# A gated attention and FFN block on one core: VectorE's order at the FFN entry, a third row buffer, and the first scores in banks of their own

## The chip, the cores and the metric

One core of a Trainium2 chip runs the kernel. The metric is the device time of one execution in microseconds. TensorE multiplies, VectorE and ScalarE read its results out of PSUM, GpSimd works on SBUF alone, SyncE issues most DMAs.

## The reference, cut to what matters

Eight batches of 100 rows of width 2048 attend to 722 context rows each, which serve as keys and as values. The result is added to x through a gate. Then a linear layer of 2048 by 2048, whose weights are packed with 6 bits each, is added through a second gate.

```python
a = einsum('bqd,bkd->bqk', layernorm(x), ctx)       # x: 8,100,2048   ctx: 8,722,2048
x = x + tanh(g_xattn[0]) * einsum('bqk,bkd->bqd', softmax(a), ctx)
w = (unpacked_6_bit(qweight) - zero_point) * scale  # 2048 x 2048
x = x + tanh(g_ffn[0]) * (einsum('bsd,nd->bsn', layernorm(x), w) + bias)
```

## The kernel before, in words

Every engine runs a program of its own, written out by hand; semaphores tie them together. What an engine does next is the order of the code in its block, and a wait at its head holds everything behind it on that engine.

**Split operands.** fp32 operands are split in a high part (rounded, made by ScalarE) and a low part (the rest, made by VectorE or GpSimd). Products are the sum of three passes: high by high, low by high, high by low.

**Attention, batch b.** `queries` turns the normalised rows of x (in `xa`) in four groups: TensorE transposes into a PSUM bank, ScalarE writes the high half of `qT` (L535), VectorE the low half (L877). `scores(b)` goes over 32 chunks f: TensorE turns three blocks of context (L980), ScalarE copies `khi` (L544), VectorE subtracts `klo` (`keys_lo`, L887), and three chunks later TensorE multiplies (L1025 with khi, L1027 with klo) into the two banks of `S`. VectorE takes the maximum (`row_max`), ScalarE the exponential (`exps`). `attend(b)` multiplies the probabilities with the context, six row tiles in the order of `ORDER` or `LAST_ORDER`, into the four `pv` banks (L1063, L1074). Its low operands `vlo` come from GpSimd (L487). VectorE adds the result to x piece by piece (`residual`, L764).
`keys_lo`, `keys_hi`, `scores`, `attend` and `multiply` take a table of hooks: other work that stands ahead of chunk or tile f. So the statistics of the next x (`ln1_stats`) stand at chunks 27 to 30 of batch 0, and the unpacking of weight tiles 0 and 1 (`unpack_piece`, five operations each) from chunk 12 on of batch 7.
The turns use four banks `T`: two of their own and, while batches 0 and 1 are loaded, `pv0` and `pv1` too. A bank is written again when its low half has been taken (`s_free`).

**FFN.** 800 rows are cut into row blocks of 128 and a tail of 32. A block m is read back from DRAM into a row buffer (`load_rows`, buffers in `XROW`), turned by TensorE in two halves of eight transposes (`normed`), copied by ScalarE (`rows_hi`, L607) and VectorE (`rows_lo`, L796). A weight tile n (128 of the 2048 outputs) is loaded (`load_w`), unpacked by VectorE (`unpack`, L817 to L824), turned by TensorE (`weights`, L1098, 16 transposes) and copied by ScalarE (L529). `multiply(nb, m)` is 16 steps of two matmuls (L1131). VectorE finishes each result tile j in two parts: `before(j)` prepares x1 (L853, L856; it needs the DMA of `load_x1` and of `rs_all`), `after(j)` combines it with the product (L868, L871).
`weights(n)` and the next `normed` share the banks T0 and T1, so TensorE's turns wait for VectorE's `rows_lo` of the block before.

**Start.** SyncE loads x[0] in four pieces, then 24 pieces of context of batch 0, x[1], and so on: all in one queue. TensorE turns the identity 34 times (L1159) before the first queries, after waiting for all masks of GpSimd.

The functions as they stand before:

## Time and profile before

| what | us |
| --- | --- |
| median of 3 runs (lowest, highest) | 606.73 (603.69, 607.91) |
| the profiled execution, its own time | 604.58 |
| its span, first to last instruction | 602.8 |
| TensorE busy | 576.8 (96%) |
| VectorE busy | 357.2 (59%) |
| ScalarE busy | 287.3 (48%) |
| GpSimd busy | 221.3 (37%) |

In the rows, PE is TensorE, PEld its weight loads, DVE VectorE, ACT ScalarE, POOL GpSimd, SPq the DMAs that SyncE issues. Lnnn is the line of the kernel. What stands in brackets is how long the engine was idle before the row and which engine or DMA ended that. PEclk is the granted TensorE clock: 1.00 is 2.4 GHz, 0.50 is 1.2 GHz.

### The profile page before, as it was taken

To read this page: it belongs to the slowest core of one execution; us is meant where nothing else is said; L and a number is where in the kernel's file an instruction comes from. 1 tells how busy PE (TensorE), PEld (TensorE's weight loads), DVE (VectorE), ACT (ScalarE), POOL (GpSimd) and SP (SyncE) were. 2 spreads that over 40 slices of the span, in tenths; PEclk is the share of its full clock that TensorE was granted. 3 is DMA by queue.
4 is the path that set the end of the run, shared out by engine and by line. 5 is a ranking of instruction groups with operands and counts; after the bars stand their busy time and mean duration, and the time that the engine had idled before them with its cause. 6 is when DMAs were issued, how large, how long until landed. Compare 5 with 4: busy or idle time off the path is not lost.

```text
span 602.8 us, 8793 instructions
## 1 busy us (share of the span) xinstructions
PE 576.8 (96%) x3458; PEld 413.1 (69%) x3458; DVE 357.2 (59%) x680; ACT 287.3 (48%) x450; POOL 221.3 (37%) x196
## 2 busy tenths in 40 slices
PE   7989999999999999999999899992999999999997
PEld 7968969968968968968968876651654444444445
DVE  5676717827827827826836946771757764654433
ACT  3755567568568568568568567441323211210000
POOL 2046178169169269269269159420000000000000
PEclk9998999999999999999999999996999999999999
DMA  7999649237847856846848485896434984972311
GB/s 231 280 271 255 202 135 316 73 114 222 226 154 223 200 184 222 232 147 229 216 159 296 108 314 211 241 261 176 151 134 140 262 242 113 207 152 62 89 53 39
DMA packets 44435, 113.69 MB, mean 189 GB/s; under 512 B 21026, under 2 KB 21282, under 8 KB 35778
## 3 DMA queue, kind: packets, MB, share of 16 engines
q1 hardware_dynamic: 27388, 108.12, 59.1%
q10 hardware_dynamic: 16750, 5.01, 5.2%
q8 instruction: 27, 0.44, 0.4%
q14 instruction: 14, 0.11, 0.1%
q0 software_dynamic: 256, 0.00, 0.0%
HBM read 89.26 MB, written 19.66 MB: 181 GB/s over the span
## 4 chain that ended last, share of the span: by engine, by line
PE 84%; DVE 6%; DMA 3%; POOL 3%; ACT 2%; issue 1%; SPq 0%; POOLq 0%; DVEq 0%; ACTq 0%
PE pv L1131 18%; PE pv L1063 13%; PE S L1025 13%; PE T L980 9%; PE S L1131 8%; PE S L1027 7%; PE pv L980 5%; PE pv L1074 5%; DVE xres L764 3%; POOL vlo L487 2%; DMA late<-x_scratch 2%; DMA raw<-in_L_ffn_qweight 1%; PE T L1098 1%; PE T L1159 1%; DVE qT L877 1%
## 5 line engine op out<-in xcount | busy, mean ns | idle before, releaser
L487 POOL TENSOR_TENSOR vlo<-raw,vhi 128x2048 fp32r<-128x2048 f32 (+1 forms) x38 | 175.4, 4644 | 50.3 <-ACT vhi L555 50.3
L1025 PE MATMUL S<-khi,qT 128*100 128x362 f32 x512 | 142.1, 359 | 2.2 <-ACT khi L544 2.2
L1027 PE MATMUL S<-klo,qT 128*100 128x362 f32 x256 | 85.8, 335 | 3.5 <-DVE klo L887 3.0
L1063 PE MATMUL pv<-vhi,ph 128*100 128x512 f32 (+1 forms) x304 | 85.4, 397 | 0.6 <-DVE xres L764 0.4
L887 DVE TENSOR_TENSOR klo<-pv,khi 128x361 fp32r<-128x361 f32 x128 | 65.1, 526 | 25.7 <-ACT khi L544 25.1
L887 DVE TENSOR_TENSOR klo<-T,khi 128x361 fp32r<-128x361 f32 x128 | 65.8, 529 | 23.2 <-ACT khi L544 22.5
L1131 PE MATMUL pv<-raw 128*128 128x512 f16 x352 | 78.0, 379 | 0.0
L544 ACT ACTIVATE khi<-T 128x361 fp32r<-128x361 f32 x128 | 58.4, 474 | 36.6 <-PE T L980 36.5
L555 ACT ACTIVATE vhi<-raw 128x2048 fp32r<-128x2048 f32 (+1 forms) x38 | 71.9, 1908 | 6.8 <-PE pv L1063 6.7
L544 ACT ACTIVATE khi<-pv 128x361 fp32r<-128x361 f32 x128 | 58.5, 476 | 28.3 <-PE pv L980 28.2
L1025 PEld LDWEIGHTS S<-khi,qT 128*100 128x100 f32 x512 | 68.3, 168 | 2.4 <-ACT E L579 2.4
L980 PE MATMUL T<-ident,raw 128*128 128x128 f32 (+2 forms) x432 | 66.7, 270 | 0.5 <-DVE qT L877 0.5
L1131 PEld LDWEIGHTS pv<-raw 128*128 128x128 f16 x352 | 34.2, 98 | 41.4 <-issue 1.7
L1063 PEld LDWEIGHTS pv<-vhi,ph 128*100 128x100 f32 (+1 forms) x304 | 49.3, 165 | 19.0 <-DVE xres L764 1.4
L980 PEld LDWEIGHTS T<-ident,raw 128*128 128x128 f32 (+2 forms) x432 | 55.7, 149 | 5.9 <-issue 1.3
L980 PE MATMUL pv<-ident,raw 128*128 128x128 f32 (+1 forms) x384 | 59.6, 266 | 0.0
L877 DVE TENSOR_TENSOR qT<-T,qT 128x400 fp32r<-128x400 f32 x28 | 14.8, 569 | 70.6 <-ACT qT L535 70.6
L980 PEld LDWEIGHTS pv<-ident,raw 128*128 128x128 f32 (+1 forms) x384 | 48.8, 140 | 3.7 <-DVE qT L877 0.7
L1027 PEld LDWEIGHTS S<-klo,qT 128*100 128x100 f32 x256 | 42.4, 166 | 8.8 <-DVE klo L887 8.2
L466 POOL TENSOR_SCALAR ln<-mr 100x1 f32<-100x1 f32 x16 | 3.7, 230 | 114.4 <-DVE mr L721 113.9
L1063 PE MATMUL pv<-vlo,ph 128*100 128x512 f32 (+1 forms) x152 | 44.6, 393 | 0.0
L626 ACT ACTIVATE xa<-raw 128x2048 f16<-128x2048 f16 x8 | 15.3, 1910 | 50.0 <-DVE raw L824 45.9
(110 smaller groups left out, 681.6 us busy)
## 6 DMA issues: line engine op xcount, KB each, us to landing
raw<-in_ctx SPq DMA_DIRECT2D x24, 1024.0 KB, 9.6
raw<-in_L_ffn_qweight SPq DMA_DIRECT2D x16, 768.0 KB, 7.2
raw<-in_ctx SPq DMA_DIRECT2D x12, 840.0 KB, 8.7
raw<-in_ctx SPq DMA_DIRECT2D x32, 256.0 KB, 10.9
xres<-in_x SPq DMA_DIRECT2D x8, 800.0 KB
x_scratch<-xres SPq DMA_DIRECT2D x8, 800.0 KB
rows_scratch<-xres SPq DMA_DIRECT2D x8, 800.0 KB
late<-x_scratch SPq DMA_DIRECT2D x24, 256.0 KB, 5.0
```

The costliest lines, as they stand in the source:

```text
L487: pool.tensor_tensor(vlo[0:r, k, :], raw[0:r, b % 2, t, :], vhi[0:r, k, :].bitcast(F32), ALU.subtract).then_inc(s_vlo, 1)
L544: act.activation(khi[:, (b * 2 * CH + f) % RING, 0:GW], T[k][:, 0:GW], ACT.Copy).then_inc(s_khi, 1)
L555: act.activation(vhi[0:ROWS[t], n % PAIRS, :], raw[0:ROWS[t], b % 2, t, :], ACT.Copy).then_inc(s_vhi, 1)
L764: dve.scalar_tensor_tensor(out=piece, in0=pv[n][0:R, :], scalar=soft[0:R, i % 2, 3:4], in1=piece, op0=ALU.mult, op1=ALU.add).then_inc(s_x1, 1)
L877: dve.tensor_tensor(qT[:, 1, 4 * f:4 * f + 4, :], T[k][:, 0:4 * R].rearrange("p (c r) -> p c r", r=R), qT[:, 0, 4 * f:4 * f + 4, :].bitcas ...
L887: dve.tensor_tensor(klo[:, slot, 0:GW], T[k][:, 0:GW], khi[:, slot, 0:GW].bitcast(F32), ALU.subtract).then_inc(s_free[k], 1)
L980: last = pe.transpose(dst(T[k]), src, ident[0:n, 0:n])
L1025: pe.matmul(S[0:R, g, 0:MW], qT[:, h, c, :], khi[:, slot, :], start=(c == 0 and h == 0), stop=False)
L1027: last = pe.matmul(S[0:R, g, 0:MW], qT[:, 0, c, :], klo[:, slot, :], start=False, stop=(c == CH - 1))
L1063: last = pe.matmul(pv[n][0:R, :], ph[0:r, p, t, :], v[0:r, k, n * 512:(n + 1) * 512], start=(first and a == 0), stop=(final and a == 2))
L1074: last = pe.matmul(pv[n][0:R, :], p, raw[0:r, b % 2, t, n * 512:(n + 1) * 512], start=False, stop=final)
L1131: last = pe.matmul(ACC[(j + k) % NA][0:r, cols], xT[m][:, h, c, :], WT[nb % 2][:, c, cols], start=(c == 0 and h == 0), stop=(c == CH - 1 a ...
```

## The change

1. **VectorE's order at the FFN entry.** `unpack(5)` now stands ahead of block 3, `shares` and `unpack(6)` ahead of block 4, and `before(0)` and `after(0)` behind block 4's first half. The residual of batch 6 stands ahead of the last low probabilities.
2. **Third row buffer.** Block 4 is read into `late[:, 2, :]`, free once attention is done (`s_pv`), and its load is issued ahead of weight tile 6. x1's first two pieces are issued ahead of `rs_all`.
3. **TensorE's order.** The weight turns in the last `attend` stand one tile later; `weights(3)` stands behind it, directly ahead of the first `multiply`.
4. **First scores in banks of their own.** Batch 0 uses `S0` (the banks of `pv2`, `pv3`), so `scores(1)` no longer waits for the first exponential. `row_max(0)` and `exps(0)` move into batch 1, at chunks 3 and 7.
5. **Statistics of x[1]** at chunks 22, 24, 26, 28 and the centring at chunk 30 of batch 0.
6. **Unpacking of tiles 0 and 1** at chunks 16 to 29 of batch 7 in place of 12 to 30.
7. **Start.** TensorE waits only for the first mask, turns the identity 30 times; two of the four pieces of x[0] are issued by ScalarE.

```diff
...
         scB, bB, cB = (consts[:, k, :] for k in range(3))
-        xrow = [xa[:, :], region(1, 2)]
...
-        XROW = [(0, 0), (0, 1), (1, 0), (0, 2), (1, 1), (0, 3), (1, 2)]
+        xrow = [xa[:, :], region(1, 2), late[:, 2, :]]
...
+        XROW = [(0, 0), (0, 1), (1, 0), (0, 2), (2, 0), (1, 1), (0, 3)]
         xT = [b.bitcast(F16).rearrange("p (h c r) -> p h c r", h=2, c=CH)
...
         S = psum("S", [P, 2, 512])
-        pv = [psum(f"pv{n}", [P, 512]) for n in range(NCH)]
...
+        S0 = psum("S0", [P, 2, 512])
+        pv = [psum(f"pv{n}", [P, 512]) for n in range(2)] + [S0[:, n, :] for n in range(2)]
...
         T = [psum(f"T{k}", [P, 512]) for k in range(2)] + pv[0:2]
-        ACC = [S[:, 0, :], S[:, 1, :]] + [b[:, :] for b in pv]
+        ACC = [S[:, 0, :], S[:, 1, :]] + [b[:, :] for b in pv[0:2]] + pv[2:]
         NA = len(ACC)
...
         s_rowsout = sem("s_rowsout")
-        s_xrow = [sem(f"s_xrow{k}") for k in range(2)]
+        s_xrow = [sem(f"s_xrow{k}") for k in range(3)]
         s_scB, s_bB, s_cB = sem("s_scB"), sem("s_bB"), sem("s_cB")
...
-            for c in range(NCH):
+            for c in (0, 2):
                 sp.dma_start(xa[0:R, piece(c)], x[0, :, piece(c)]).then_inc(s_xa0[c], 16)
...
                     sp.wait_ge(s_turned[k], u + 1)
+                elif m == 4:
+                    sp.wait_ge(s_pv, B * NCH)
                 elif XROW[m][1]:
...
             load_w(RT + 1)
+            load_rows(4)
             load_w(RT + 2)
             x1_out(LAST)
+            for j in range(2):
+                load_x1(j)
             sp.wait_ge(s_rsout, 16 * LAST)
...
                          allow_slow_non_contiguous=True).then_inc(s_rsin[0], 16)
-            load_rows(4)
-            for j in range(2):
-                load_x1(j)
             rows_out(LAST)
...
                 act.wait_ge(s_nmax, b + 1)
-                act.activation(E[0:R, :, :], S[0:R, :, 0:GW], ACT.Exp, bias=soft[0:R, b % 2, 0:1],
+                act.activation(E[0:R, :, :], (S if b else S0)[0:R, :, 0:GW], ACT.Exp, bias=soft[0:R, b % 2, 0:1],
                                scale=scale[0:R, b:b + 1] if b < 2 else 1.0, accum_out=soft[0:R, b % 2, 1:2]).then_inc(s_exp, 1)
...
+            for c in (1, 3):
+                act.dma_start(xa[0:R, c * 512:(c + 1) * 512], x[0, :, c * 512:(c + 1) * 512]).then_inc(s_xa0[c], 16)
             queries(0)
...
             act.dma_start(xa[0:R, :], x[2]).then_inc(s_xa, 16)
-            exps(0)
-            act.wait_ge(s_gate, 32)
-            act.activation(tg[:, 0:2], gates[:, :], ACT.Tanh).then_inc(s_tanh, 1)
...
+            def first_exps():
+                exps(0)
+                act.wait_ge(s_gate, 32)
+                act.activation(tg[:, 0:2], gates[:, :], ACT.Tanh).then_inc(s_tanh, 1)
...
             for i in range(LAST):
                 between = {}
+                if i == 0:
+                    between[7] = first_exps
                 if i >= 1:
...
                 nmax = soft[0:R, b % 2, 0:1]
+                scores = S if b else S0
                 if b >= 2:
-                    dve.tensor_reduce(nmax, S[0:R, :, 0:GW], AX.XY, ALU.max, negate=True).then_inc(s_nmax, 1)
+                    dve.tensor_reduce(nmax, scores[0:R, :, 0:GW], AX.XY, ALU.max, negate=True).then_inc(s_nmax, 1)
                 else:
-                    dve.tensor_reduce(nmax, S[0:R, :, 0:GW], AX.XY, ALU.max, negate=True).then_inc(s_max, 1)
+                    dve.tensor_reduce(nmax, scores[0:R, :, 0:GW], AX.XY, ALU.max, negate=True).then_inc(s_max, 1)
                     dve.wait_ge(s_max, b + 1)
...
             queries_lo(0)
-            keys_lo(0, {27 + c: lambda c=c: ln1_stats(1, c) for c in range(NCH)})
-            centred(1)
+            hooks = pieces_of(1, 22, 2)
+            hooks[30] = lambda: centred(1)
+            keys_lo(0, hooks)
             queries_lo(1)
-            row_max(0)
             for i in range(LAST):
...
                 else:
-                    hooks = {12 + 10 * n + 2 * k: lambda n=n, k=k: unpack_piece(n, k) for n in range(2) for k in range(5)}
+                    hooks = {16 + (15 * n + 3 * k) // 2: lambda n=n, k=k: unpack_piece(n, k) for n in range(2) for k in range(5)}
                 if i == 0:
-                    hooks[8] = first_coef
+                    hooks[3] = lambda: row_max(0)
+                    hooks[13] = first_coef
                 keys_lo(i + 1, hooks)
...
             rows_lo(0, 1)
+            residual(LAST - 1)
             probs_lo(LAST)
-            residual(LAST - 1)
             ln2_stats(LAST - 1)
...
             rows_lo(2, 0)
-            shares()
             rows_lo(2, 1)
-            before(0)
+            unpack(RT + 1)
             rows_lo(3, 0)
             rows_lo(3, 1)
-            unpack(RT + 1)
+            shares()
+            unpack(RT + 2)
+            rows_lo(4, 0)
+            before(0)
             after(0)
-            rows_lo(4, 0)
+            rows_lo(4, 1)
             before(1)
             after(1)
-            rows_lo(4, 1)
-            unpack(RT + 2)
+            unpack(RT + 3)
             before(2)
             after(2)
-            unpack(RT + 3)
             before(3)
...
             def scores(b, between={}):
+                into = S if b else S0
                 for f in range(2 * CH + AHEAD):
...
                         if e == 0:
-                            if b >= 1:
+                            if b >= 2:
                                 pe.wait_ge(s_exp, b)
...
                         for h in range(2):
-                            pe.matmul(S[0:R, g, 0:MW], qT[:, h, c, :], khi[:, slot, :], start=(c == 0 and h == 0), stop=False)
+                            pe.matmul(into[0:R, g, 0:MW], qT[:, h, c, :], khi[:, slot, :], start=(c == 0 and h == 0), stop=False)
                         written("S", b, e)
-                        last = pe.matmul(S[0:R, g, 0:MW], qT[:, 0, c, :], klo[:, slot, :], start=False, stop=(c == CH - 1))
+                        last = pe.matmul(into[0:R, g, 0:MW], qT[:, 0, c, :], klo[:, slot, :], start=False, stop=(c == CH - 1))
                 last.then_inc(s_scores, 1)
...
             def weights(n):
+                if n == 0:
+                    pe.wait_ge(s_id, 2)
                 pe.wait_ge(s_u, n + 1)
...
                 pe.wait_ge(s_parts, nb + 1)
+                if nb == 0:
+                    pe.wait_ge(s_fold, 1 + STRIPS)
                 pe.matmul(ACC[j % NA][0:TAIL, :], fold[:, 0:TAIL], parts, start=True, stop=True).then_inc(s_y, 1)
...
-            pe.wait_ge(s_id, 2)
-            pe.wait_ge(s_fold, 1 + STRIPS)
-            pe.wait_ge(s_pad, 2)
...
-            for _ in range(34):
+            pe.wait_ge(s_id, 1)
...
+            for _ in range(30):
                 pe.transpose(T[0][:, 0:P], ident[:, :], ident[:, :])
             queries(0)
+            pe.wait_ge(s_pad, 2)
             scores(0)
...
                     attend(i, {3: lambda: normed(0, (0, 1)), 4: lambda: normed(0, (2, 3)), 5: lambda: probs(LAST)})
-            attend(LAST, {0: lambda: weights(0), 1: lambda: weights(1), 2: lambda: normed(1, (0, 1)),
-                          3: lambda: normed(1, (2, 3)), 4: lambda: weights(2), 5: lambda: weights(3)})
+            attend(LAST, {1: lambda: weights(0), 2: lambda: weights(1), 3: lambda: normed(1, (0, 1)),
+                          4: lambda: normed(1, (2, 3)), 5: lambda: weights(2)})
+            weights(3)
             multiply(0, 0, {5: lambda: normed(2, (0, 1)), 11: lambda: normed(2, (2, 3))})
...
             multiply(0, 2, {3: lambda: normed(4, (0, 1)), 7: lambda: weights(RT + 1), 11: lambda: normed(4, (2, 3))})
...
```

VectorE at the FFN entry, in the kernel before (L796 is a low half of a row block, L841 `shares`, L853 and L856 `before(0)`; T0 and T1 are banks; the last four rows are block 3):

```order
L796 TENSOR_TENSOR raw<-T0,raw 128x512
L796 TENSOR_TENSOR raw<-T1,raw 128x512
L841 SCALAR_TENSOR_TENSOR consts<-consts 128x2048
L796 TENSOR_TENSOR raw<-T0,raw 128x512
L796 TENSOR_TENSOR raw<-T1,raw 128x512
L853 SCALAR_TENSOR_TENSOR late<-consts,rs_all,late 128x512
L856 TENSOR_TENSOR late<-late,consts 128x512
L796 TENSOR_TENSOR late<-T0,late 128x512
L796 TENSOR_TENSOR late<-T1,late 128x512
L796 TENSOR_TENSOR late<-T0,late 128x512
L796 TENSOR_TENSOR late<-T1,late 128x512
```

and in the kernel after (the same operations are L808, L853, L865 and L868 there, and L829, L833, L836 are an unpacking):

```order
L808 TENSOR_TENSOR late<-T0,late 128x512
L808 TENSOR_TENSOR late<-T1,late 128x512
L808 TENSOR_TENSOR late<-T0,late 128x512
L808 TENSOR_TENSOR late<-T1,late 128x512
L853 SCALAR_TENSOR_TENSOR consts<-consts 128x2048
L829 TENSOR_SCALAR raw<-raw 128x512
L833 TENSOR_SCALAR raw<-raw 128x512 x3
L836 TENSOR_SCALAR raw<-raw 128x512
L808 TENSOR_TENSOR raw<-T0,raw 128x512
L808 TENSOR_TENSOR raw<-T1,raw 128x512
L865 SCALAR_TENSOR_TENSOR late<-consts,rs_all,late 128x512
L868 TENSOR_TENSOR late<-late,consts 128x512
```

The first four rows are block 3, the next is `shares`, then come `unpack(6)` and the first half of block 4. `before(0)` went from ahead of block 3 to the last two rows here; `unpack(5)` stands directly ahead of the first row.

TensorE at the end of the last `attend`, before (L1098 is a weight tile, L1063 and L1074 are attention, L1131 is the first `multiply`):

```order
L980 MATMUL T<-ident,xa 128x128 x8
L1074 MATMUL pv<-raw,E 100x512 x4
L1098 MATMUL T<-ident,raw 128x128 x16
L1063 MATMUL pv<-vhi,ph 100x512 x4
L1063 MATMUL pv<-vlo,ph 100x512 x4
L1063 MATMUL pv<-vhi,ph 100x512 x4
L1098 MATMUL T<-ident,raw 128x128 x16
L1074 MATMUL pv<-raw,E 100x512 x4
L1131 MATMUL S<-raw 128x512 x10
```

and after (L1114, L1077, L1088 and L1147 there):

```order
L1077 MATMUL S<-vhi,ph 100x512 x2
L1077 MATMUL pv<-vlo,ph 100x512 x2
L1077 MATMUL S<-vlo,ph 100x512 x2
L1077 MATMUL pv<-vhi,ph 100x512 x2
L1077 MATMUL S<-vhi,ph 100x512 x2
L1114 MATMUL T<-ident,raw 128x128 x16
L1088 MATMUL pv<-raw,E 100x512 x2
L1088 MATMUL S<-raw,E 100x512 x2
L1114 MATMUL T<-ident,raw 128x128 x16
L1147 MATMUL S<-raw 128x512 x10
```

The last weight tile now stands directly ahead of the first `multiply`; before, four matmuls of attention (L1074) stood between the two. (The names leave buffer numbers out, so S stands for S0 as well.)

VectorE in chunks 20 to 31 of batch 0, after (L899 is the low half of a chunk, L724 the statistics of x[1], L748 the centring; before, the statistics stood at chunks 27 to 30 and the centring behind chunk 31):

```order
L899 TENSOR_TENSOR klo<-T,khi 128x361 x2
L724 BN_STATS stats<-xa 100x6
L899 TENSOR_TENSOR klo<-pv,khi 128x361 x2
L724 BN_STATS stats<-xa 100x6
L899 TENSOR_TENSOR klo<-T,khi 128x361 x2
L724 BN_STATS stats<-xa 100x6
L899 TENSOR_TENSOR klo<-pv,khi 128x361 x2
L724 BN_STATS stats<-xa 100x6
L732 BN_AGGR mr<-stats 100x2
L899 TENSOR_TENSOR klo<-T,khi 128x361 x2
L748 TENSOR_SCALAR xa<-xa,mr 100x2048
L899 TENSOR_TENSOR klo<-pv,khi 128x361 x2
```

The first statistics, which need x[1], stand in front of the low half of chunk 22.

## Rows read from the trace of the kernel before

**Rows 1.** Waits of TensorE, whole run: us in total, times, longest us

```profile
PE T L1098 <- DVE late L796: 11.3, 1, 11.3
```

**Rows 2.** Order of time, 403 to 420: start us, us, engine, line, operation, out<-in

```profile
403.50 1.12 SPq L374 DMA_DIRECT2D late<-x_scratch  x2
...
417.19 0.75 DVE L853 SCALAR_TENSOR_TENSOR late<-consts,rs_all,late 128x512 f32<-128x512 f32 x1 [13.51 <-DMA late<-x_scratch]
...
419.41 1.87 PE L1098 MATMUL T<-ident,raw 128*128 128x128 f16 x16 [11.33 <-DVE late L796]
```

**Rows 3.** Chain that ended last, 369 to 434: start us, us, engine, tile, line, count

```profile
369.64 2.73 DVE xres L764 x4
...
374.74 0.91 PE T L1098 x16
375.65 2.80 PE pv L1063 x12
...
395.30 2.16 PE S L1131 x10
397.46 0.95 PE T L980 x8
...
433.19 0.95 PE T L980 x8
```

**Rows 4.** Stretches of time: us, busy us by engine (count), PEclk, DMA share, GB/s

```profile
419.30:422.00 2.70, 2.59 (x19) 2.07 (x20) 0.56 (x1) 1.54 (x2) 0.00 (x0) 0.50 0.38 143
46.40:50.00 3.60, 3.57 (x14) 3.16 (x15) 2.31 (x5) 1.77 (x5) 3.60 (x2) 0.54 0.82 246
```

**Rows 5.** DMA issues of 389:394, 396:405 and 4:5.5: count, KB, us to landing

```profile
raw<-in_L_ffn_qweight SPq DMA_DIRECT2D x2, 768.0 KB, 13.0
...
raw<-rows_scratch SPq DMA_DIRECT2D x1, 1024.0 KB, 14.7
...
raw<-in_ctx SPq DMA_DIRECT2D x1, 210.0 KB, 8.0
```

**Rows 6.** Order of time on GpSimd, ScalarE and VectorE, 355 to 393

```profile
355.55 23.06 POOL L487 TENSOR_TENSOR vlo<-raw,vhi 128x2048 fp32r<-128x2048 f32 x5
...
391.42 1.94 ACT L529 ACTIVATE raw<-T 128x1024 f16<-128x1024 f16 x2 [1.79 <-PE T L1098]
...
392.17 1.33 DVE L821 TENSOR_SCALAR raw<-raw 128x512 uint16<-128x512 uint16 x3
```

**Rows 7.** Order of time, last scores, 331 to 334

```profile
331.33 2.07 DVE L817 TENSOR_SCALAR raw<-raw 128x512 uint16<-128x512 uint16 x1 [2.09 <-DMA raw<-in_L_ffn_qweight]
...
333.89 0.41 PE L1027 MATMUL S<-klo,qT 128*100 128x362 f32 x1 [2.17 <-DVE klo L887]
```

**Rows 8.** Order of time, start, 3 to 12

```profile
3.46 6.66 PE L1159 MATMUL T<-ident 128*128 128x128 f32 x34 [3.46 <-POOL fold L453]
...
7.22 0.69 DVE L713 BATCH_NORM_STATS2 stats<-xa 100x6 f32<-100x512 f32 x1 [0.23 <-DMA xa<-in_x]
...
8.25 1.67 DVE L737 TENSOR_SCALAR xa<-xa,mr 100x512 f32<-100x512 f32 x4
...
11.76 0.92 PE L980 MATMUL T<-ident,raw 128*128 128x128 f32 x6 [0.27 <-DVE qT L877]
```

**Rows 9.** Order of time, end of the first scores, 28 to 41

```profile
28.19 1.08 DVE L887 TENSOR_TENSOR klo<-T,khi 128x361 fp32r<-128x361 f32 x2
...
33.52 0.69 DVE L713 BATCH_NORM_STATS2 stats<-xa 100x6 f32<-100x512 f32 x1 [0.21 <-DMA xa<-in_x]
...
40.53 0.91 PE L980 MATMUL T<-ident,xa 100*128 100x100 f32 x8 [0.74 <-DVE xa L737]
```

**Rows 10.** Order of time, TensorE in the second scores, 46 to 52

```profile
46.43 0.70 PE L1025 MATMUL S<-khi,qT 128*100 128x362 f32 x2 [2.16 <-ACT khi L544]
...
50.48 0.56 PE L1025 MATMUL S<-khi,qT 128*100 128x362 f32 x2
...
51.30 0.55 PE L1025 MATMUL S<-khi,qT 128*100 128x362 f32 x2
```

## Prediction

> **What bounds the kernel now.** I read the page first: TensorE is busy for 576.8 of 602.8 us (table above), so only its remaining 26 us and the time at the lower clock can be won. Next the waits of TensorE: one of 11.3 us on VectorE's L796 dwarfs the rest [rows 1]. Then the order of time around it. VectorE stands from 403.7 to 417.19 at L853, before(0), for a 256 KB piece of x1 issued at 403.50; behind it in VectorE's order are the low halves of row block 3, and TensorE's third weight tile (L1098) needs the banks that they free. It runs at 419.41 [rows 2]. Its 16 turns then take 1.87 us where they take 0.91 elsewhere [rows 2, 3]: after standing idle, TensorE works 2.6 us at a granted clock of 0.50, the 1.2 GHz level [rows 4].
>
> **The FFN entry: 12.2 us.** From the chain of work: a tile of weights (16 turns) lasts 0.91 us, half a row block (8 turns) 0.95, a multiply step of two matmuls 0.43 [rows 3]. From the first multiply at 395.30 to the second turn of block 4 the work is 6.9 (16 steps) + 1.9 (block 2) + 6.9 + 1.9 (block 3) + 0.9 (tile) + 4.8 (11 steps) + 0.95 + 0.9 = 25.2 us, which would end at 420.5. That turn stood at 433.19 [rows 3]. So 12.7 us are lost: 11.3 in the wait, 1.3 in the half-clock stretch.
> In the changed order VectorE does block 2, unpack(5), block 3, shares, unpack(6), the first half of block 4, and only then before(0). What is late next? unpack(5) needs weight tile 5, whose load is issued when unpack(3) is done, about 392.7 by the next part; the two loads of that kind took a median 13.0 us [rows 5], so it lands near 405.7. An unpacking is one operation of 0.5, three in 1.33 and one of 0.3 us, 2.0 with gaps [rows 6]. VectorE ends unpack(5) at 407.8 and the first half of block 3 (1.3 us) at 409.1, where TensorE asks for its banks (396.3 + 6.9 + 1.9 + 3.0 + 0.95). That is just in time. shares takes about 2.2 us and unpack(6) 2.0, both after block 3 (413.8): 418.0; the first half of block 4 then ends at 419.3, where TensorE would want its banks, one after the other, from 418.5: a new wait of 0.5 us. Block 4's rows go into the third buffer: issued about 393.7 (attention done) instead of 401.98, with the same 14.7 us [rows 5] they are there at 408.4, and are needed at 416. x1's first piece, issued at about 398.3, with 14.7 us lands at 413, before 419.3. So of 12.7 us, 0.5 come back: **12.2 won**. Bounds: tile 5 with the slowest row's 14.7 us gives 1.3 more of a wait; with that and a whole weight load (2 us at the spacing of those loads) queued ahead, 3.5 more.
>
> **The handover before it: a loss of 1.0.** The last batch's first tile waits piece by piece for the residual (L764, 369.64 and 2.73 long) and ends at 374.74; its 12 matmuls last 2.80 [rows 3], so with the 0.91 of a weight tile ahead it could have ended near 372.5: 2.2 lost. The residual now runs ahead of the last low probabilities, which hides it. But the tiles' vlo come from GpSimd's row of five (355.55, 23.06 us: the third ends at 369.4, the fourth at 374.0) [rows 6]. Tile 0 then runs from 369.4 to 372.2, weights(0) to 373.1, and TensorE stands until 374.0 for tile 1, which begins 1.6 us before it did (375.65 [rows 3]). From there the work is the same except that one weight tile (0.9) now comes behind it, so all would be done at 394.4. The price is there: weights(3) now stands directly ahead of multiply(0,0), which needs all tiles copied. ScalarE's two copies last 0.97 us each (1.94 for two) [rows 6]. Before, a tile of matmuls covered them; now nothing does, and the second copy ends at about 396.3. The multiply starts **1.0 us later**. Bounds: 0 to 1.9 (both copies bare).
>
> **The last scores: 2.2 us.** At chunk 12 of batch 7 VectorE waits for weight tile 0, landing at 331.3, and its first operation takes 2.07 us beside GpSimd; TensorE pays 2.17 us at L1027 [rows 7]. Begun at chunk 16, that is 4 steps of 0.81 us later (spacing of the L1025 rows at 50.48 and 51.30 [rows 10]), it finds the tile there. The ten pieces at 0.42 us each (2.0 + gaps for five) and 15 low halves at 0.5 make 11.7 us in 15 steps of 12.2 us: they fit. **2.2 won**; bounds 0 and 2.2.
>
> **The start: a new wait inside.** Four parts.
> (a) The warm-up turns started at 3.46, after all masks, and ran 6.66 us to 10.12, past the first centred piece (8.25 + 0.42) [rows 8]. With 30 turns from about 1.9 they end near 8; the first query turn starts at 8.7 instead of 9.95. The first context turn moves from 11.76 [rows 8] to about 10.6. The limit is context: three pieces issued from 4.0 to 5.5 took up to 8.0 us [rows 5], so some 12 to 13.4, needed 2.2 us after 11.76 before. Worth 1.1 us; bounds 0 and 1.2.
> (b) Two of x's four pieces go to ScalarE's queue. The last piece landed at 7.2 [rows 8]; from two queues it could land earlier. I take nothing. The Trainium skill (DMA: Bandwidth & Descriptors, "Issuing engines are not separate DMA queues") says that both queues feed the same 16 engines and interleave, so a second issuer adds no bandwidth; this speaks against the edit, since context pieces now mix with x's. By it the sum stays as it is. Without it the sum stays too: (a) would start earlier and meet the context limit.
> (c) Statistics of x[1] move from chunks 27 to 30 to chunks 22 to 28. But x[1] landed only at 33.5: VectorE waited for it even at chunk 27 [rows 9]. The low half of chunk 21 ends at 29.27, now 28.2; there VectorE stands until 33.5, with chunk 22's low half behind the wait. TensorE's L1027 of chunk 22 would run at 30.5, and gets its operand at 34.6: **4.1 us of waiting**, and probably the half clock after it, as in the two stretches of rows 4. From 33.5 VectorE then has four statistics of 0.6, ten low halves of 0.5, aggregate and centring (1.5) in one chain, and 0.6 us where chunk 27 waits for ScalarE: 43.0 for the last low half, so queries(1) starts at 43.1 where it started at 40.53 [rows 9]. That is 2.6 later.
> (d) Given back: scores(1) no longer waits for exp(0). Before, its first matmul came at 46.43 after 2.16 us idle [rows 10], and 3.6 us at a clock of 0.54 followed [rows 4], so that chunk 4 came at 51.30, 4.9 us after, where 4 steps are 3.2. Now the first matmul comes at about 46.9 (queries 43.1 + 3.8, which is 2.6 later than the 44.3 at which the turns were done), with the clock up, and chunk 4 at 50.2. The maximum (1.1 us at chunk 3) and the exponential (1.3 us at chunk 7) lie in the slack of three chunks ahead. Net of (a), (c), (d): **1.1 won**. Bounds: with no wait for x[1], 1.1 + 2.16 + 1.6 = 4.9 won; with no head start and a second half-clock stretch, 1.6 lost.
>
> **Sum.** 12.2 - 1.0 + 2.2 + 1.1 = 14.5 us. The profiled execution took 604.58 us (span 602.8), so 590.1. The median of the three runs is 606.73, 2.15 above it, which would give 592.2. I forecast 591.0, between them; the rivals are counted from it.
>
> **Rivals.**
> 1. The wait for x[1] does not bite (x lands early, or the slack swallows it): up to 3.8 us more, 587.2. For it: VectorE waited only 0.21 us at chunk 27. Against: at chunk 22 it comes 5 us sooner. 0.12.
> 2. The start loses: after 4.1 us idle the clock stays at 0.50 longer and drops again at the queries; 2.7 us less, 593.7. For it: both idle stretches were followed by that level [rows 4]. Against: 2.16 us of idle cost only 1.6. 0.15.
> 3. A new wait stands in the place of the old: weight tile 5 lands late, unpack(5) blocks the low halves of block 3 just as before(0) did. For it: loads issued there take 13.0 to 14.7 us [rows 5] and I left it no slack. Price 3 to 6 us: 595.5. 0.14.
> 4. Slower than before: in that same place, the change does not do what it says. The DMA engines are backlogged while block 3, tile 5, block 4 and tile 6 queue up, and VectorE stands at unpack(5). TensorE loses one us for each us after 406.3; the gain of 14.5 is gone when tile 5 lands at 421, 28 us after its issue; with a landing at 424 the time is 591.0 + 17.7 = 608.7. Against: the slowest row there is 14.7 us. 0.02.
>
> **How the numbers follow.** Forecast 0.57, rivals 0.12, 0.15, 0.14, 0.02. The range runs from rival 1 (587.2) past rival 2 to the upper part of rival 3 plus the 1 us between profile and median: 586.5 to 597.5. A measurement of this kernel tells about 1% (6 us) from no change. Faster by over 1% (under 600.7): the forecast, rivals 1 and 2 and nearly all of 3, 0.94; within 1%: 0.04; slower: 0.02.
>
> **What would show it.** In the profile after: TensorE's 11.3 us wait gone and no 0.50 clock near 410 to 420; VectorE's wait of 3 to 5 us for x at the first chunk statistics near 28 to 33, and TensorE's wait of about 4 us at the S<-klo line there; no wait over 0.5 us in the last scores; a gap of 1 to 1.6 us between weights(3) and the first multiply; before(0) not waiting for its DMA. Wrong would be: a wait over 2 us at the second or third weight tile of the FFN block, or a start that reaches chunk 4 of batch 1 before 48 or after 52 us.

## The result, and the profile after

The changed kernel takes **590.6 us** (median of 4, 588.2 to 593.3; the kernel before beside it 606.3). The ratio is 0.974, 95% interval 0.969 to 0.979. The prediction was 591.0, with 586.5 to 597.5 as its range. The four executions are two pairs, though: 588.32 and 588.21 with a mean granted clock of 0.999, 593.29 and 592.88 with 0.994. No execution took 591. The profiled one took 588.32 us, its span is 586.5.

TensorE's waits, whole run of the kernel after (us in total, times, longest us):

```profile
PE S L1041 <- DVE klo L899: 3.4, 3, 2.4
PE T L993 <- DVE xa L748: 2.4, 1, 2.4
PE T L1175 <- POOL ident L452: 1.7, 1, 1.7
PE S L1147 <- issue: 1.6, 1, 1.6
...
PE T L1114 <- DVE raw L808: 0.2, 1, 0.2
```

The 11.3 us of [rows 1] are gone. The first row is new in this place: the wait for the low half behind the statistics of x[1]. The second has grown from 0.7 us: queries(1) wait for the centring of x[1]. The fourth is the bare copy ahead of the first multiply. The last is the wait that took the place of the 11.3.

The FFN entry in order of time, kernel after (start us, us, engine, line, operation, what it was idle for), which answers to [rows 2]:

```profile
397.30 0.32 SPq L367 DMA_DIRECT2D late<-rows_scratch  x1
397.67 0.43 SPq L354 DMA_DIRECT2D raw<-in_L_ffn_qweight  x1
...
401.26 0.52 DVE L829 TENSOR_SCALAR raw<-raw 128x512 uint16<-128x512 uint16 x1 [1.95 <-DMA raw<-in_L_ffn_qweight]
...
414.10 1.13 PE L1114 MATMUL T<-ident,raw 128*128 128x128 f16 x16 [0.18 <-DVE raw L808]
418.53 0.75 DVE L865 SCALAR_TENSOR_TENSOR late<-consts,rs_all,late 128x512 f32<-128x512 f32 x1 [3.98 <-DMA rs_all<-rs_scratch]
```

Weight tile 5 landed at 401.2, and its unpacking waited for it. before(0) (L865) still waits 4 us for a DMA, but now nothing urgent stands behind it. The row block for the third buffer was issued only at 397.3: SyncE stands there for 8.7 us until the store of batch 6's rows (800 KB, issued at 384.1) has landed, at 397.2. In every kernel that issues it there, block 4 goes out 0.1 us or less behind that store.

The start, same kernel, which answers to [rows 8 to 10]:

```profile
1.66 5.08 PE L1175 MATMUL T<-ident 128*128 128x128 f32 x30 [1.66 <-POOL ident L452]
...
7.57 0.69 DVE L724 BATCH_NORM_STATS2 stats<-xa 100x6 f32<-100x512 f32 x1 [0.79 <-DMA xa<-in_x]
...
32.17 0.69 DVE L724 BATCH_NORM_STATS2 stats<-xa 100x6 f32<-100x512 f32 x1 [3.64 <-DMA xa<-in_x]
33.36 0.41 PE L1041 MATMUL S<-klo,qT 128*100 128x362 f32 x1 [2.35 <-DVE klo L899]
...
41.48 0.85 PE L993 MATMUL T<-ident,xa 100*128 100x100 f32 x8
...
44.93 0.56 PE L1039 MATMUL S<-khi,qT 128*100 128x362 f32 x2
```

and the same stretch by granted clock (columns: stretch, us, TensorE busy, count, PEclk, DMA share, GB/s):

```profile
27.00:50.00 23.00, 19.33 (x141) 1.00 0.99 277
```

x[1] landed at 32.2 and not at 33.5, TensorE waited 2.35 us and not 4.1, and the clock stayed at its full level. The last piece of x[0] (7.57) came 0.35 us later than before, with two issuing queues. x[1] itself was issued at 15.09 instead of 16.04, since SyncE has two transfers fewer ahead of it.

**Where the time went.** Two marks cut every profile in three: chunk 4 of batch 1 (fifth khi matmul group of scores(1)) and the first multiply of the FFN block.

| kernel | start to chunk 4 | to first multiply | to the end | span |
| --- | --- | --- | --- | --- |
| before | 51.3 | 343.8 | 207.7 | 602.8 |
| after | 48.2 | 342.8 | 195.5 | 586.5 |
| gained | 3.1 | 1.0 | 12.2 | 16.3 |
| predicted | 1.1 | 1.2 | 12.2 | 14.5 |
| vector order undone | 52.5 | 343.0 | 209.0 | 604.5 |
| vector order alone | 51.6 | 343.9 | 196.4 | 591.9 |
| two row buffers | 48.4 | 343.0 | 198.6 | 590.0 |
| statistics late | 48.4 | 343.1 | 197.7 | 589.2 |
| shared banks | 52.5 | 343.0 | 201.1 | 596.5 |
| last sum write later | 52.5 | 343.0 | 195.8 | 591.3 |
| sum writes by ScalarE | 49.1 | 343.0 | 195.9 | 588.0 |
| unpacking from 12 | 53.4 | 346.8 | 195.2 | 595.4 |
| pieces on SyncE | 50.9 | 343.1 | 196.8 | 590.7 |
| late, pieces on SyncE | 47.4 | 343.0 | 197.2 | 587.5 |
| late, tile 6 first | 48.7 | 343.0 | 197.8 | 589.4 |
| sums in one row | 48.0 | 343.1 | 195.2 | 586.3 |

(Profiled executions; the rows below the fourth are the experiments.)

### The profile page after: what moved, and what is told of

Same layout as the page of the kernel before. It is cut to its first block, busy times and chain, and to the rows that moved or that the text cites. A ratio compares the mean times of both kernels' runs of the same rounds, so it can differ in the third digit from the quotient of the medians.

```text
span 586.5 us, 8784 instructions
## 1 busy us (share of the span) xinstructions
PE 571.8 (97%) x3454; PEld 409.1 (70%) x3454; DVE 356.3 (61%) x680; ACT 287.3 (49%) x450; POOL 219.3 (37%) x196
## 4 chain that ended last, share of the span: by engine, by line
PE 82%; DVE 6%; POOL 3%; DMA 3%; SPq 2%; issue 1%; ACT 1%
PE S L1147 19%; PE S L1039 12%; PE T L993 9%; PE pv L1147 8%; PE S L1041 7%; PE pv L1077 6%; PE S L1077 6%; PE pv L993 5%; POOL vlo L491 3%; DMA xa<-in_x 3%; DVE xres L776 3%; PE pv L1088 3%; PE S L1088 3%; SPq L326 2%; PE T L1114 1%
## 5 line engine op out<-in xcount | busy, mean ns | idle before, releaser
L899 DVE TENSOR_TENSOR klo<-pv,khi 128x361 fp32r<-128x361 f32 x128 | 65.3, 527 | 23.5 <-ACT khi L548 22.9
L899 DVE TENSOR_TENSOR klo<-T,khi 128x361 fp32r<-128x361 f32 x128 | 65.7, 528 | 21.3 <-ACT khi L548 20.4
L1147 PE MATMUL S<-raw 128*128 128x512 f16 x320 | 71.7, 379 | 1.6 <-issue 1.6
L993 PE MATMUL T<-ident,raw 128*128 128x128 f32 (+1 forms) x416 | 63.9, 268 | 0.4 <-DVE qT L889 0.3
L1147 PEld LDWEIGHTS S<-raw 128*128 128x128 f16 x320 | 31.0, 98 | 38.4 <-ACT raw L533 1.8
L993 PEld LDWEIGHTS T<-ident,raw 128*128 128x128 f32 (+1 forms) x416 | 53.2, 145 | 5.2 <-issue 0.7
L1077 PE MATMUL pv<-vhi,ph 128*100 128x512 f32 (+1 forms) x152 | 49.6, 400 | 1.2 <-POOL vlo L491 0.6
L1077 PE MATMUL S<-vhi,ph 128*100 128x512 f32 (+1 forms) x152 | 48.5, 393 | 0.0
L880 DVE TENSOR_TENSOR late<-S,consts 128x512 f32<-128x512 f32 (+2 forms) x19 | 12.8, 674 | 49.6 <-PE S L1147 49.6
L1147 PE MATMUL pv<-raw 128*128 128x512 f16 x192 | 42.6, 379 | 0.0
## 6 DMA issues: line engine op xcount, KB each, us to landing
raw<-in_ctx SPq DMA_DIRECT2D x32, 256.0 KB, 10.4
```

The source lines that it names most:

```text
L899: dve.tensor_tensor(klo[:, slot, 0:GW], T[k][:, 0:GW], khi[:, slot, 0:GW].bitcast(F32), ALU.subtract).then_inc(s_free[k], 1)
L993: last = pe.transpose(dst(T[k]), src, ident[0:n, 0:n])
L1077: last = pe.matmul(pv[n][0:R, :], ph[0:r, p, t, :], v[0:r, k, n * 512:(n + 1) * 512], start=(first and a == 0), stop=(final and a == 2))
L1147: last = pe.matmul(ACC[(j + k) % NA][0:r, cols], xT[m][:, h, c, :], WT[nb % 2][:, c, cols], start=(c == 0 and h == 0), stop=(c == CH - 1 a ...
```

## Experiments

Times are medians, each with its ratio to the kernel before on the same chip; the kernel after has 0.974 (0.969 to 0.979).

### 1. VectorE's order undone, and alone

```diff
             rows_lo(2, 0)
+            shares()
             rows_lo(2, 1)
-            unpack(RT + 1)
+            before(0)
             rows_lo(3, 0)
             rows_lo(3, 1)
-            shares()
-            unpack(RT + 2)
-            rows_lo(4, 0)
-            before(0)
+            unpack(RT + 1)
             after(0)
```

> The changed kernel with VectorE's order at the FFN entry as before (before(0) ahead of block 3, unpack(5) behind it); the third buffer, SyncE's order and TensorE's order stay. Theory (VectorE's order carries nearly all of the 12.2 us): before(0) again stands at its DMAs with block 3's low halves behind it, TensorE waits 10 to 16 us at the third weight tile, and the median is 601 to 607 us. In the changed kernel the small load of rs_all landed only at 418.5, so the wait may now hang on it rather than on x1. Rival (x1's two pieces ahead of rs_all on SyncE and the third buffer carry most of it): wait under 5 us, median 591 to 595.

606.9 us (11 runs), ratio 1.000 (0.997 to 1.003): this part undone, the rest gives nothing that can be measured. VectorE and TensorE in the run with the order undone:

```profile
418.74 0.75 DVE L865 SCALAR_TENSOR_TENSOR late<-consts,rs_all,late 128x512 f32<-128x512 f32 x1 [14.94 <-DMA rs_all<-rs_scratch]
...
420.97 1.87 PE L1114 MATMUL T<-ident,raw 128*128 128x128 f16 x16 [12.50 <-DVE late L808]
```

The old wait is back, though x1 was issued earlier: it now ends with the 2.5 KB of rs_all (418.65), x1's first piece being there at 418.0. The FFN part costs 13.5 us more (209.0 against 195.5). Another 4.3 us were lost at the start, which the edit doesn't touch; experiment 3 finds that cause. The rival falls.

The reverse edit (the same lines, changed in the kernel before):

> The kernel before with only VectorE's order at the FFN entry changed (block 3 and both unpackings ahead of before(0)); two row buffers, SyncE's order, TensorE's order, start and first scores as before. Theory (this order is the main cause by itself): the 11.3 us wait goes, block 4 is read at 402 and lands near 417, some 3 us before it is needed at 420; 11 to 12.5 us less than before, 594 to 596. Rival A (the third buffer or x1's earlier place is needed with it): block 4 lands late or weight tile 6 behind it does, a wait of 3 us or more at the turn of block 4 or the third weight tile, and only 5 to 9 us less, 598 to 602. Rival B (undoing the order cost 16 us in the changed kernel, so it alone gives 16): 591.

599.4 us (593.7 to 599.6, 5 runs), ratio 0.985 (0.979 to 0.991). The profiled execution, 593.72, is the lowest: its FFN part is 196.4, 11.3 us better than before, and what is missing is one wait for block 4, issued at 402.62 as in the kernel before:

```profile
416.75 1.23 PE L980 MATMUL T<-ident,raw 128*128 128x128 f32 x8 [1.27 <-DMA raw<-rows_scratch]
```

So the theory holds for the execution that was seen, and rival A's number for the median, which is only 6.3 us under the kernel before beside it (605.8). Three of the five took 599.4 to 599.6 at clocks of 0.989 to 0.991 (0.997 in the profiled one); no profile shows where, so that stays open.

### 2. Two row buffers

```diff
-        xrow = [xa[:, :], region(1, 2), late[:, 2, :]]
+        xrow = [xa[:, :], region(1, 2)]
-        XROW = [(0, 0), (0, 1), (1, 0), (0, 2), (2, 0), (1, 1), (0, 3)]
+        XROW = [(0, 0), (0, 1), (1, 0), (0, 2), (1, 1), (0, 3), (1, 2)]
```

> The changed kernel with two row buffers again: block 4 goes to the buffer of block 2 and its load waits until block 2 is turned; its place on SyncE stays that of the changed kernel. Theory (the third buffer gives nothing by itself: in the changed kernel that load was issued only at 397.3, when SyncE came round to it, about when block 2 has been turned): within 1 us of the changed kernel, 589.5 to 591.5, block 4 turned at the same time after the first multiply (25.8 us to its second turn). Rival (the buffer is needed for the early load): a wait of 2 to 5 us at the turn of block 4, 593 to 596.

594.5 us (588.9 to 595.6), ratio 0.976 (0.973 to 0.980). The median is outside what the theory expected and within the rival's range, but the interval overlaps that of the kernel after. The rival's wait at the turn of block 4 doesn't show in the profile. The FFN part is 3.1 us longer there, and the largest piece of it is tile 5, landed 11.8 us after the first multiply began (10.2 in the kernel after):

```profile
PE T L1112 <- DVE late L806: 1.0, 1, 1.0
```

Two smaller waits (0.3 us at block 2, 0.4 at block 5) stand beside it, and over 1 us of the 3.1 has no wait that the profile shows. The buffer's own worth is not settled; in the seen execution it is not needed for the early load: block 4 was issued at 399.86, and what SyncE waited for was again the store of batch 6's rows, landed at 399.80.

### 3. The start

(a) Statistics of x[1] late:

```diff
-            hooks = pieces_of(1, 22, 2)
-            hooks[30] = lambda: centred(1)
-            keys_lo(0, hooks)
+            keys_lo(0, {27 + c: lambda c=c: ln1_stats(1, c) for c in range(NCH)})
+            centred(1)
```

> The changed kernel with the statistics of x[1] back at chunks 27 to 30 and the centring behind the last low half. Theory (the early place costs a wait of 3.64 us on VectorE and 2.35 us on TensorE, and in half of the executions a stretch at 1.2 GHz behind it, which is why the runs fall into two groups, near 588.3 with a clock of 0.999 and near 593.1 with 0.994): no wait over 0.5 us at the S<-klo line near 33 us, all runs with a clock of 0.999 and within 1 us of each other at 586.5 to 588.5, so 2 to 4 us under the changed kernel's median. Rival A (the two groups come from elsewhere, such as the clock at the very start): the two groups stay, both some 1 to 2 us lower. Rival B (the early statistics earn their place, since queries(1) no longer wait for centring): 590.5 to 593, and a wait of 1 to 3 us at the queries near 42.

589.2 us (587.2 to 591.2), ratio 0.970 (0.967 to 0.973); no clock under 0.996. The wait was 1.6 us at most, not under 0.5, because x[1] came late here:

```profile
35.48 0.69 DVE L724 BATCH_NORM_STATS2 stats<-xa 100x6 f32<-100x512 f32 x1 [2.89 <-DMA xa<-in_x]
...
36.66 0.41 PE L1040 MATMUL S<-klo,qT 128*100 128x362 f32 x1 [1.59 <-DVE klo L899]
```

The landing records tell why. The trace has eleven of them for x[1]: one 0.8 to 1.8 us after its issue, and ten as its parts land (the expectations count all eleven as parts). In the kernel after the ten are there by 32.2. Here nine are there by 33.9 and the last at 35.5; with the vector order undone nine by 32.2 and the last at 35.5. With early statistics such a landing is expensive. The run with the last sum write held back, whose start is that of the kernel after:

```profile
35.77 0.69 DVE L726 BATCH_NORM_STATS2 stats<-xa 100x6 f32<-100x512 f32 x1 [7.40 <-DMA xa<-in_x]
```

```profile
27.00:50.00 23.00, 16.64 (x108) 0.85 0.97 257
```

VectorE stands 7.4 us, TensorE 6.1, the clock falls to its 1.2 GHz level (0.85 over the stretch), and chunk 4 comes at 52.5 instead of 48.2. Its time (593.06) and clock (0.994) are those of the upper pair of the kernel after. By chunk 4 (profiles with the first scores in their own banks): early statistics, x[1] by 33.0: 48.0 to 49.1 (four profiles); x[1] at 34.2 to 36.2: 50.9 to 53.4 (four); late statistics, x[1] at 34.4 to 35.5: 47.4 to 48.7 (three). **The early place gains nothing when x[1] is on time and loses 3 to 5 us when it isn't.** (Late statistics with x[1] on time were not met.) That the upper pair of the kernel after is this case is inferred from clock and time and not shown: it has no profile of its own, and executions of 592.0 to 593.3 at 0.994 also occur with late statistics (experiments 3c and 6), whose profiled starts lose nothing of the kind; so a late weight tile remains as a rival.

(b) Is it the second queue that delays x[1]?

```diff
-            for c in (0, 2):
+            for c in range(NCH):
                 sp.dma_start(xa[0:R, piece(c)], x[0, :, piece(c)]).then_inc(s_xa0[c], 16)
-            for c in (1, 3):
-                act.dma_start(xa[0:R, c * 512:(c + 1) * 512], x[0, :, c * 512:(c + 1) * 512]).then_inc(s_xa0[c], 16)
```

> The changed kernel with all four pieces of x[0] issued by SyncE again. Four of the eight profiles with two pieces on ScalarE's queue show one of the eleven parts of x[1] landing 3 us after the others (35.4 to 36.5 instead of 32.1 to 32.5), a wait of 5.8 to 6.4 us at the S<-klo line and 4.2 us more; the two profiles with all pieces on SyncE don't. Theory (the second queue brings that about): the late part is gone, every run has a clock of 0.999 or 1.0, median 587.5 to 589. Rival A (it comes from elsewhere, and two profiles were too few to meet it): two groups again, 588 and 593. The last piece of x[0] lands at 7.2 instead of 7.5 and the first query turn starts 0.3 us earlier in either case; by my term b of the start nothing else changes.

592.8 us (591.6 to 600.2), ratio 0.980 (0.975 to 0.985). The theory falls: two of the ten parts landed at 34.2, TensorE waited 4.47 us, chunk 4 came at 50.9. The first query turn starts 0.5 us earlier (8.64 against 9.14).

(c) Both together:

> The changed kernel with the statistics of x[1] back at chunks 27 to 30 and all pieces of x[0] on SyncE. Theory (the late statistics make the start safe against the late part of x[1], whatever causes it; the queue of x[0] adds little): 586.5 to 588.5 median, no run over 590 save those where a weight tile is late in the FFN block, and the best of all kernels. Rival (with x[1] at 33.5 both places are the same and only the FFN block's spread is left): 588 to 590, not to be told from the changed kernel's lower group.

589.5 us (586.9 to 592.5), ratio 0.972 (0.969 to 0.976); the profiled start is the best of all (chunk 4 at 47.4 with x[1] at 34.4), but two executions took 592. It isn't told apart from the kernel after.

(d) First scores back in the shared banks:

```diff
-                            if b >= 2:
+                            if b >= 1:
                                 pe.wait_ge(s_exp, b)
...
-                into = S if b else S0
+                into = S
```

> The changed kernel with the first scores back in the banks that all batches share, so scores(1) waits for exp(0) again; everything else stays. Theory (the own banks give what term d says): a wait of 2.2 to 2.5 us at the first multiply of scores(1), followed by a stretch near 0.50 of the clock, chunk 4 of batch 1 at 51.5 to 52.5 instead of 48.2, and 3 to 4 us more: 592 to 595. Rival (the three chunks ahead swallow the wait, as the queries now end 1 us later too): under 1 us more, 590.5 to 591.6.

595.7 us (592.8 to 598.5), ratio 0.980 (0.976 to 0.983), 0.7 above the theory's range. Start and FFN entry of that run:

```profile
47.75 0.90 PE L1036 MATMUL S<-khi,qT 128*100 128x362 f32 x2 [2.16 <-ACT khi L548]
```

```profile
47.70:52.00 4.30, 4.25 (x20) 0.62 0.93 236
```

```profile
PE T L1111 <- DVE raw L805: 4.4, 1, 4.4
```

The wait and the low clock of [rows 4, 10] are back: chunk 4 at 52.5, 4.3 us later. Of these 2.2 are the wait, 1.5 the low clock behind it, and 0.7 were lost ahead of it. The last row was not expected. Weight tile 6 landed at 419.8, 23 us after its issue, and cost 5.6 us of FFN time (201.1 against 195.5). That is my rival 3, one tile later.

### 4. The last scores

```diff
-                    hooks = {16 + (15 * n + 3 * k) // 2: lambda n=n, k=k: unpack_piece(n, k) for n in range(2) for k in range(5)}
+                    hooks = {12 + 10 * n + 2 * k: lambda n=n, k=k: unpack_piece(n, k) for n in range(2) for k in range(5)}
```

> The changed kernel with the unpacking of weight tiles 0 and 1 back at chunks 12 to 30 of batch 7. Theory (the prediction's term for the last scores): VectorE stands 2 us at the first piece for the DMA, TensorE waits 2.0 to 2.3 us at the S<-klo line near 329 to 333, and the time is 2.2 us more in either group: 590.5 and 595. Rival (the tile is loaded by then because SyncE runs a little further ahead; or the wait is swallowed): under 0.7 us more.

594.3 us (592.9 to 597.2), ratio 0.980 (0.975 to 0.985).

```profile
333.77 1.83 DVE L829 TENSOR_SCALAR raw<-raw 128x512 uint16<-128x512 uint16 x1 [2.35 <-DMA raw<-in_L_ffn_qweight]
336.09 0.41 PE L1041 MATMUL S<-klo,qT 128*100 128x362 f32 x1 [2.17 <-DVE klo L899]
```

```profile
336.00:345.00 9.00, 8.91 (x54) 0.81 0.74 178
```

The wait is back to the hundredth. The middle part grew by 4.0 (346.8 against 342.8; 3.8 against the 343.0 of most others) and not by 2.2, since 1.2 GHz followed: 9 us at 0.81 lose 1.7. In the kernel before, the same wait was followed by the full clock. So this term is worth 2.2, or nearly 4.

### 5. What makes the weight tiles late

In all profiles the landings near 400 spread when GpSimd's 400-byte write of the row sums (100 rows of 4 bytes) is under way. Three edits test it. First, hold the last of them back:

```diff
+                if i == LAST:
+                    pool.wait_ge(s_w[0], 16 * 4)
                 pool.dma_start(rs_dram[i * R:(i + 1) * R, :], rneg[0:R, i % 2:i % 2 + 1]).then_inc(s_rsout, 16)
```

> The changed kernel, with GpSimd's last write of row sums (400 bytes of rs_scratch, issued at 401.1) held back until weight tile 6 has landed. Theory (tile 6, x1's first pieces and rs_all share the 16 DMA engines with that small write while it is under way, from 405.6 to 415.1 in the changed kernel, and a transfer caught by it needs about 10 us from its first part to its last; in the run with shared banks it caught tile 6, whose last part came at 419.9, TensorE waited 4.4 us and 1.2 GHz followed): tile 6 lands within 2 us from first part to last, rs_all and x1's first pieces are there before 414 instead of 418, and of the timed runs none has a wait at the third weight turn; median 588 to 591, lowest 587.5 to 588.3. Rival A (that write is innocent, the engines are merely backlogged by the 1 MB row block and the 768 KB tile): rs_all and x1 still land near 418, the spread of the times is as before. Rival B (the 593 group of the changed kernel comes from x[1] landing late at the start, not from here): the two groups stay, 588 and 593, since this edit doesn't touch the start.

593.0 us (588.1 to 596.6), ratio 0.976 (0.969 to 0.982). The write now lands from 413.6 to 424.6, and rs_all takes 4.1 us from its first part to its last (411.0 to 415.1) instead of 11.9 (406.6 to 418.4). Weight tile 7 is the one beside the write, with 12.7 us instead of 7.1. The median doesn't fall. The one execution with a profile lost its time at the start, as rival B said; the five times (588.1, 590.0, 593.0, 593.1, 596.6) are not its two groups, and what the others lost is open.

Second, ScalarE issues the last two of them (one more semaphore, and two waits for it):

> The changed kernel, with the last two writes of row sums (400 bytes each) issued by ScalarE instead of GpSimd, at about the same time. Theory (it is GpSimd's own kind of DMA that makes them slow and slows others): they land within 2 to 3 us, the 1 MB and 768 KB loads beside them in under 10 us, weight tile 5 lands by 399 instead of 401.2; median 588 to 590. Rival (any write of 100 rows of 4 bytes behaves so): 7 to 10 us from first part to last again, tile 5 at 401, median 588 to 593 in two groups.

589.2 us (588.1 to 594.2), ratio 0.972 (0.966 to 0.979). rs_all still takes 9.2 us from first part to last, tile 5 still 6.8, and lands at 401.1; the two writes themselves take 11.3 and 11.4. The issuing queue isn't the cause.

Third, one row of 400 bytes in place of 100 rows of 4:

```diff
+            row = ident[0:1, 0:R].bitcast(F32)
...
-                pool.dma_start(rs_dram[i * R:(i + 1) * R, :], rneg[0:R, i % 2:i % 2 + 1]).then_inc(s_rsout, 16)
+                pool.dma_start(rs_dram[i * R:(i + 1) * R, :].rearrange("r o -> o r"), row).then_inc(s_rsout, 16)
```

> The changed kernel, with each write of row sums (100 rows of 4 bytes, one from each partition) replaced by one row of 400 bytes from a single partition. The sums themselves are not written, a row of the identity is, so the term of the zero points is left out of the result; order, waits and all other transfers stay. Theory (it is the many 4-byte elements that need 7 to 10 us and slow what is beside them): that write lands within 1 us from first part to last, weight tile 5 needs 3 to 5 us from first part to last instead of 8.0, rs_all and x1's first pieces 3 to 5 us instead of 12, and are there by 411; with no late tile the median is 588 to 590.6. Rival (the 1 MB and 768 KB loads queue up behind each other, the small write is only their victim): tile 5 still takes 8 us, rs_all and x1 still 10 to 12 us.

590.7 us (588.2 to 592.5), ratio 0.974 (0.971 to 0.978). DMA from 384 to 402 (in the rows of issues: count, KB, us to landing), kernel after:

```profile
DMA packets 580, 3.71 MB, mean 206 GB/s; under 512 B 86, under 2 KB 86, under 8 KB 257
...
raw<-in_L_ffn_qweight SPq DMA_DIRECT2D x2, 768.0 KB, 11.5
xa<-rows_scratch SPq DMA_DIRECT2D x1, 1024.0 KB, 14.6
...
late<-x_scratch SPq DMA_DIRECT2D x2, 256.0 KB, 19.0
rs_scratch<-rneg POOLq DMA_DIRECT2D x2, 0.4 KB, 12.8
rs_all<-rs_scratch SPq DMA_DIRECT2D x1, 2.5 KB, 18.4
```

and with the sums in one row:

```profile
DMA packets 1192, 5.49 MB, mean 305 GB/s; under 512 B 369, under 2 KB 369, under 8 KB 744
...
raw<-in_L_ffn_qweight SPq DMA_DIRECT2D x3, 768.0 KB, 9.7
...
xa<-rows_scratch SPq DMA_DIRECT2D x1, 1024.0 KB, 9.6
...
late<-x_scratch SPq DMA_DIRECT2D x4, 256.0 KB, 10.4
...
rs_scratch<-ident POOLq DMA_DIRECT2D x2, 0.4 KB, 6.9
rs_all<-rs_scratch SPq DMA_DIRECT2D x1, 2.5 KB, 11.4
```

Every load in these rows is faster. The packets of the main queue fill 83% of the 16 engines' time in the kernel after and 87% here, yet 206 GB/s moved there and 305 here: the engines were no less busy, they moved less. The Trainium skill (DMA: Bandwidth & Descriptors, "Why small descriptors are slow (HBM only)") says that each descriptor carries a fixed overhead however small it is; the write's first to last part, 5.4 to 11.4 us as 100 rows and 2.0 to 4.7 as one, agrees in direction; whether that overhead is large enough, no run here shows. That other transfers beside it slow down as much as this it doesn't say; the rows show it. Tile 5 needs 3.6 us from first part to last instead of 8.0 (6.5 to 10.4 in the other thirteen profiles), rs_all 5.4 instead of 11.9. Block 4 goes out at 390.77 instead of 397.30, since the store of batch 6's rows that it waits for lands at 390.7 and not at 397.2. The write itself is slower than I said (under 1 us). One more thing bears on rs_all: in all fourteen profiles its last part lands 0.3 to 1.7 us behind the last part of another 800 KB store, the one of x1 issued 1.6 to 7.7 us ahead of it (416.8 in the kernel after, 403.9 here). So the small write may hold up rs_all by way of that store; which of the two, the runs don't separate. No time is won: where the FFN entry has no late tile there is nothing to win (195.2 against 195.5).

### 6. Weight tile 6 ahead of block 4

```diff
-            load_rows(4)
             load_w(RT + 2)
+            load_rows(4)
```

(with the late statistics)

> The changed kernel with the late statistics, and weight tile 6 issued ahead of row block 4 on SyncE. Theory (what is left of the spread is the race between weight tiles 5 and 6 and GpSimd's last small write): tile 6 lands 1 to 3 us earlier and always before that write begins, block 4 lands at 406 to 408 and is needed at 412; no wait over 0.5 us in the FFN block beside the 1.6 at its head; median 586.5 to 588. Rival (block 4 is now the transfer that is caught, lands at 415 and TensorE waits 2 to 3 us for it): 589 to 591.

591.2 us (586.6 to 593.3), ratio 0.974 (0.970 to 0.978). Tile 6 is there at 406.3 (406.6 in the kernel after, 409.9 in the profile of the late statistics alone), block 4 only at 410.9 but in time. The wait is at tile 5, which this order doesn't move: 1.69 us, landing 12.6 us after the first multiply began. Both guesses of the time miss.

## Why the prediction was right

**The FFN entry: as reckoned.** Predicted 12.2, measured 12.2 (207.7 - 195.5). The new wait at the third weight tile is 0.2 us where I had 0.5. In the profiled executions VectorE's order alone carries 11.3 of it, and undone takes 13.5 away; by the medians the order alone gives 6.3 us and undone takes 16, of which the profile has 4.3 at the start. Three details were wrong. "before(0) not waiting for its DMA": it waited 3.98 us, for rs_all and not for x1, without harm since its new place has slack. Block 4 issued at 393.7, when attention is done: it was 397.3, also in time. It waits for the store of batch 6's rows too, a wait that the prediction left out. Tile 5 at 405.7 with "no slack": that was right, in a timetable 4 us earlier. It landed 10.2 us after the first multiply began (I had 9.4); where it took 11.5 to 12.6 (two row buffers, pieces on SyncE, tile 6 first) TensorE waited 1.0 to 1.7 us. With the statistics late, tile 4 was late instead (landed 0.7 us before the first multiply, 3.5 in the kernel after) and TensorE waited 1.5 us at the turn of block 2.

**Handover and last scores: +1.2 predicted, +1.0 measured.** The gap of 1.63 us ahead of the first multiply stands where it was put. The wait in the last scores is gone; with its 2.2 us the handover alone lost 1.2, for 1.0 forecast.

**The start: the term that was mis-sized.** I took 1.1 us, the profiled execution gained 3.1. The step that failed is (c), "There VectorE stands until 33.5": x[1] landed at 32.2, so TensorE waited 2.35 us and not 4.1, queries(1) came at 41.48 and not 43.1, and no half clock followed. Part (a) gave 0.8 (first context turn at 11.00 against 11.76), not 1.1, as the last piece of x[0] was 0.35 us later; (b) was right to take nothing for x[0]: that a second issuing engine adds no bandwidth, as the Trainium skill has it (DMA: Bandwidth & Descriptors, "Issuing engines are not separate DMA queues"), agrees with the trace, where the last piece even came later. What it left out is x[1], issued 0.95 us earlier behind two transfers fewer. In the ten profiles with two pieces on ScalarE the ninth of x[1]'s ten parts is there at 31.7 to 33.9 (median 32.3), in the four with all on SyncE at 33.0 to 34.2 (33.5), so the 1.3 us by which (c) was out come in part, it seems, from (b); no run isolates this. Part (d) was right: undone, it costs 4.3 us, of which 2.2 and 1.5 are the wait and the low clock, for 2.16 + 1.6 reckoned.

**The median was met partly by luck.** My start, with a wait of 4.1 us and a half clock, lies between the two kinds that the profiles show. By their times, half the executions are near rival 1 (587.2; "x lands early"), half near rival 2 (593.7; the clock stays low after the wait), and 591.0 is the middle of these pairs. Rivals 1 and 2 were rated 0.12 and 0.15 as if one would be true; if the upper pair is the late x[1], which isn't shown, they take turns. Rival 3 exists too, seen once in full (tile 6, 5.6 us).

**Best version.** None is shown to beat the changed kernel: 0.970 (0.967 to 0.973) with late statistics against 0.974 (0.969 to 0.979) overlap. The lowest single times, 586.6 to 587.2, are all from kernels with the late statistics.

## What to carry to other kernels

Undo the main part alone: here it showed at once that without one reordering of VectorE nothing of the gain is left. Before counting on an earlier load, list everything that its issue waits for: here a store of 800 KB, and not the buffer, set it. Order an in-order engine by when its results are needed, and ask of each operation that waits for a DMA what stands behind it; moved early, it gains nothing when the data is on time and costs its full delay when one part is late. When timed executions form two groups, compare the three or four marks of several profiles before explaining the median, and don't take a group for explained that has no profile.

## What the runs showed of the hardware that was not expected

- A write of 100 rows of 4 bytes slows the loads beside it. rs_all (2.5 KB) took 4.1 and 5.8 us from first part to last where all or most of it ran ahead of that write (write held back, kernel before), 9.0 to 14.1 beside it (eleven profiles). As one row of 400 bytes the write lets a 768 KB tile land in 3.6 us from first part to last instead of 8.0. Issued by ScalarE it is no better.
- One or two of the ten parts of x[1] can land 0.9 to 3.3 us after the rest, in seven of the fourteen profiles, with one issuing queue or two. The cause is open.
- A wait of TensorE of the same length can leave the clock at 2.4 GHz or be followed by 1.2: 2.17 us in the last scores (1.00 before, 0.81 with the unpacking at chunk 12), and 2.35 at the start against 2.43 (1.00 after, a fall with two row buffers). What decides it is open.
